# A graph layer with attention and experts: a prologue with other statistics, another load order and other places for the padding records

## What is computed

```
xn = layernorm(x)                                          # per row, over 512
x  = x + gnn(xn, src, dst, ...) + mix(xn)                  # mix: 8-head linear attention, softmax of q and of k
x  = x + experts(layernorm(x))                             # router, top 2 of 8 experts
# gnn: 40,000 edges
xs, xv  = xn[:, :128] @ W_in2f_s, xn[:, 128:] (3 x 128) @ W_in2f_v   # the node table
h       = shifted_softplus(f_ij @ Wf1 + bf1)               # f_ij: 20 features of the edge
W       = (h @ Wf2 + bf2) * rcut
message = products of xs[idx_j], xv[idx_j], u = r_ij/|r_ij| and W
agg     = segment_sum(message, idx_i)                      # idx_i = src: 1250 receiving nodes, unsorted
```

## Time and profile before

| | |
|---|---|
| median of 3 runs | 1466.07 us (1460.82 to 1468.56) |
| profiled execution, device time | 1465.51 us |
| its span | 1463.8 us |
| busy: PE, DVE, ACT, POOL | 1270.0, 1148.5, 819.3, 922.6 us |
| granted TensorE clock, mean | 0.938 |

### The profile page before, as it was taken

The page is one execution under the profiler, slowest core; times in us unless marked ns, Lnnn a source line. Parts: engine busy times, 40 slices in busy tenths (PEclk is TensorE's granted clock), DMA queues, the critical chain, the costliest instruction groups (busy, mean ns, idle before and its releaser), DMA issues.

```text
span 1463.8 us, 16076 instructions
## 1 busy us (share of the span) xinstructions
PE 1270.0 (87%) x4215; PEld 731.3 (50%) x4215; DVE 1148.5 (78%) x2117; ACT 819.3 (56%) x1777; POOL 922.6 (63%) x834
## 2 busy tenths in 40 slices
PE   3968878889888888699999999999999998885993
PEld 2655556666666655334444444444444443674871
DVE  6876547777777798569999999999999998367325
ACT  2355545666666656146667666666767655454330
POOL 7336666666666667568888888888888842143215
PEclk8979889999999999999999999999999999987995
DMA  8116656656656866588888888888888854434447
GB/s 247 49 66 249 238 200 249 244 201 256 243 223 258 311 210 237 210 303 292 306 297 297 290 294 298 298 306 297 299 293 292 286 175 121 173 130 169 162 130 213
DMA packets 104542, 344.51 MB, mean 235 GB/s; under 512 B 16501, under 2 KB 17437, under 8 KB 94469
## 3 DMA queue, kind: packets, MB, share of 16 engines
q0 software_dynamic: 58496, 192.21, 37.6%
q1 hardware_dynamic: 45956, 151.29, 28.3%
HBM read 216.63 MB, written 126.80 MB: 235 GB/s over the span
## 4 chain that ended last, share of the span: by engine, by line
PE 70%; DVE 12%; issue 6%; ACT 4%; another core or an unknown queue 4%; POOL 2%; DMA 2%; DVEq 0%; ACTq 0%; POOLq 0%
PE PS L2040 20%; PE PS L2045 18%; PE PS L1976 12%; PE PS L2165 5%; DVE RR L1350 3%; PE PS L1854 2%; PE PS L1935 2%; PE PS L1864 1%; PE PS L1943 1%; PE PS L1917 1%; POOL expert_inputs L832 1%; ACT RR L1029 1%; PE PS L2184 1%; PE PS L1974 1%
## 5 line engine op out<-in xcount | busy, mean ns | idle before, releaser
L799 POOL DMA_INDIRECT RR<-node_table,RR x332 | 470.6, 1418 | 144.3 <-issue 92.5
L1029 ACT ACTIVATE RR<-RR 128x256 f32<-128x256 f32 x996 | 407.2, 494 | 227.8 <-PE PS L2045 195.9
L783 POOL DMA_INDIRECT edge_records<-RR x316 | 325.8, 1031 | 190.3 <-issue 83.1
L2040 PE MATMUL PS<-RR 128*125 128x512 f32 x664 | 303.6, 599 | 20.2 <-issue 11.1
L2045 PE MATMUL PS<-RR 128*125 128x512 f32 x664 | 299.3, 592 | 0.0
L1350 DVE TENSOR_TENSOR RR<-PS,RR 128x512 f32<-128x512 f32 x237 | 161.8, 686 | 127.7 <-PE PS L1976 74.7
L2040 PEld LDWEIGHTS PS<-RR 128*125 128x125 f32 x664 | 117.8, 187 | 199.9 <-issue 186.2
L2045 PEld LDWEIGHTS PS<-RR 128*125 128x125 f32 x664 | 124.6, 188 | 160.3 <-issue 160.3
L1976 PE MATMUL PS<-wf_high,h_high 128*128 128x512 f32 x316 | 155.7, 493 | 22.0 <-DVE RR L1350 13.1
L1523 DVE TENSOR_TENSOR RR<-RR 128x1536 f32<-128x1536 f32 (+1 forms) x88 | 145.9, 1658 | 0.0
L1976 PE MATMUL PS<-wf_low,h_high 128*128 128x512 f32 x316 | 131.4, 416 | 0.0
(11 more groups left out here) (338 smaller groups left out, 1884.4 us busy)
## 6 DMA issues: line engine op xcount, KB each, us to landing
RR<-edge_records SPq DMA_DIRECT2D x78, 1040.0 KB
expert_inputs<-RR SPq DMA_DIRECT2D x8, 2560.0 KB
RR<-in_L_ffn_beta_w SPq DMA_DIRECT2D x8, 1024.0 KB
expert_w_raw<-in_L_ffn_expert_w SPq DMA_DIRECT2D x8, 1024.0 KB, 7.3
expert_outputs<-RR SPq DMA_DIRECT2D x27, 256.0 KB
edge_records<-RR POOLq DMA_INDIRECT x332
RR<-node_table,RR POOLq DMA_INDIRECT x332
RR<-edge_records SPq DMA_DIRECT2D x10, 520.0 KB
```

Source lines behind the costliest of these rows:

```text
L783: g.indirect_dma_start(out=rec_dram, out_offset=place, in_=ST[:, j, :], in_offset=None).then_inc(scattered[c], 16)
L799: g.indirect_dma_start(out=GB[:, q % GBS, t, 1:5, :].rearrange("p k n -> p (k n)"), out_offset=None, in_=tab_dram, in_offset=bass.Indirect ...
L1029: last = a.activation(message_slot(q)[:, t, k:k + 5:4, :], GB[:, q % GBS, t, 0:k + 3:k + 2, :], ACT.Copy, scale=record_slot(q)[:, t, 4 * C ...
L2040: te.matmul(PS[0:NT, b, :], OH[:, q % OHS, t, 0:NT], GB[:, q % GBS, t, 1:5, :].rearrange("p k n -> p (k n)"), start=(t == 0), stop=(t == n ...
```

## The change

- x is loaded in three parts: tiles 0 and 1, tiles 2 to 5 ahead of WV, tiles 6 to 9 behind WV.
- For tiles 2 to 9 ScalarE takes the statistics: a Copy with scale -1/512 whose accumulator gives minus the mean, and a Square with that as bias whose accumulator gives 512 times the variance. The square root then scales and adds epsilon. VectorE takes the reciprocals for tiles 2 and 3, 4 and 5, 6 to 9 apart.
- The masks of `count_block` are kept (`block_mask`), and COUNT_TILE is 7.
- `list_pairs` becomes `places_in_blocks`: ten operations on the kept masks in place of 19.
- `add_base` and POOL's share of it are gone. ScalarE makes for each tile a diagonal matrix of its offsets, and TensorE adds up ten products diagonal times mask in one PSUM bank, after the ten tiles of x; `pair_places` adds that bank once.
- `spare_places` moves from VectorE to POOL (without is_ge and the reduction), ahead of all scatters. Nine padding scatters come ahead of step 0, the other seven at steps 10, 20, ..., 70.
- The order ahead of step 0 differs on ScalarE, VectorE and TensorE, as below.

```diff
+        in_hidden = 4 * 512 // RC1
+        mask_at = [hidden_at + b * RC1 if b < in_hidden else kn_at + (b - in_hidden) * RC1 for b in range(NB)]
+        offset_diag = [w[:, 0:P] for w in (tC, tD)]
+        OFFSET_BANK = 6
+        block_mask = [R1[:, w:w + RC1] for w in mask_at]
-        COUNT_TILE = 4
+        COUNT_TILE = 7
-        EMPTY_STEP = 2
+        SPARE_FIRST = 9
+        spare_step = [10 * (n + 1) for n in range(NCOL - LOOPED - SPARE_FIRST)]
   # SP
+            load_x(slice(2, 6), x_in[1])
             load_projection(WV, Wv, wqkv_in[2])
-            load_x(slice(2, NB), x_in[1])
+            load_x(slice(6, NB), x_in[2])
   # POOL
-            pool.wait_ge(pairs_placed, 1)
-            for b in range(NB // 2, NB):
-                dest = tD if b > NB // 2 else tC
-                step(g.tensor_scalar(dest, bkt, float(b), off[:, b:b + 1], ALU.is_equal, ALU.mult))
-                if b > NB // 2:
-                    step(g.tensor_tensor(tC, tC, tD, ALU.add))
-            pool.sem_inc(pairs_listed, 1)
-            pool.wait_ge(places_ready, 1)
+            def spare_places():
+                pool.wait_ge(spare_bases, 1)
+                step(g.tensor_tensor(passed, kd.unsqueeze(2).to_broadcast([P, SPARE, 2 * NB]),
+                                     cpad.unsqueeze(1).to_broadcast([P, SPARE, 2 * NB]), ALU.subtract))
+                step(g.tensor_scalar(passed, passed, 0.0, 1.0, ALU.max, ALU.min))
+                step(g.tensor_tensor(passed, passed, fill.unsqueeze(1).to_broadcast([P, SPARE, 2 * NB]), ALU.mult))
...
+                g.tensor_copy(posi[:, RC1:NCOL], pd[:, 1:SPARE]).then_inc(places_ready, 1)
+            spare_places()
+            for n in range(SPARE_FIRST):
+                spare_record(LOOPED + n)
             for m in range(STEPS):
                 scatter(m // RING, m % RING)
-                if EMPTY_STEP <= m < EMPTY_STEP + NCOL - LOOPED:
-                    spare_record(LOOPED + m - EMPTY_STEP)
+                if m in spare_step:
+                    spare_record(LOOPED + SPARE_FIRST + spare_step.index(m))
   # ScalarE
+            def moments_of(ts):
+                for t in ts:
+                    a.activation(b2_rows[0:NT, :], X[0:NT, t, :], ACT.Copy, scale=-1.0 / D,
+                                 accum_out=mean[0:NT, t:t + 1]).then_inc(moments, 1)
+                for t in ts:
+                    act.wait_ge(moments, t - 1)
+                    a.activation(bb[0:NT, :], X[0:NT, t, :], ACT.Square, bias=mean[0:NT, t:t + 1],
+                                 accum_out=var_eps[0:NT, t:t + 1]).then_inc(squares, 1)
             table_rows(0)
+            act.wait_ge(x_in[1], 32)
+            moments_of((2, 3))
+            later_std(slice(2, 4), 3)
+            moments_of((4, 5))
+            later_std(slice(4, 6), 5)
             values(0)
             table_rows(1)
+            evac_xT(2)
             values(1)
-            std_of(slice(2, NB), 1)
-            act.wait_ge(nrm_sq, 1)
-            a.activation(inv, ssq, ACT.Sqrt).then_inc(nrm_root, 1)
-            evac_xT(2)
+            act.wait_ge(x_in[2], 32)
+            moments_of((6, 7))
             for t in range(2, NB):
                 table_rows(t)
                 if t + 1 < NB:
                     evac_xT(t + 1)
+                if t == 2:
+                    moments_of((8, 9))
+                    later_std(slice(6, NB), NB - 1)
                 values(t)
-                if t == 4:
+                if t == 5:
+            def offset_diagonal(b):
+                if b >= 2:
+                    act.wait_ge(diag_used, b - 1)
+                a.activation(offset_diag[b % 2], ident[:, :], ACT.Copy, scale=off[:, b:b + 1]).then_inc(diag_ready, 1)
+            act.wait_ge(spare_bases, 1)
+            for b in range(NB):
+                offset_diagonal(b)
...
             log_part(0, 0)
+            log_part(0, 1)
+            act.wait_ge(diag_used, NB)
+            high(0, 0)
             stage_f(3)
             radial(0, 2)
-            log_part(0, 1)
             stage_f(4)
             radial(0, 3)
             log_part(0, 2)
-            high(0, 0)
   # VectorE
-            for t in range(3):
-                count_block(t)
-            statistics(range(2, NB), 1)
-            inverse_root(range(2, NB), 1)
+            count_block(0)
+            inverse_root(range(2, 4), 1)
             normal(2)
             normal(3)
...
+                        step(v.scalar_tensor_tensor(srcf, block_mask[b], packed[:, b:b + 1], srcf, ALU.mult, ALU.add))
...
             def stage(i, c):
+                if (i, c) == (0, 0):
+                    dve.wait_ge(places_ready, 1)
...
             stage_f_low(0, 2)
+            hidden(0, 0)
             pair_places()
+            hidden(0, 1)
             stage_f_low(0, 3)
-            hidden(0, 0)
-            spare_places()
-            hidden(0, 1)
-            stage_f_low(0, 4)
             dve.wait_ge(b2_ready, 1)
             low(0, 0)
+            stage_f_low(0, 4)
   # TensorE, after the ten tiles
+            for b in range(NB):
+                pe.wait_ge(diag_ready, b + 1)
+                te.matmul(PS[:, OFFSET_BANK, 0:RC1], offset_diag[b % 2], block_mask[b], start=(b == 0), stop=(b == NB - 1))\
+                    .then_inc(diag_used, 1)
...
             layer1(0, 0)
+            layer1(0, 1)
             transposes(0, 2)
-            layer1(0, 1)
             transposes(0, 3)
```

More of the change, by code:

```diff
@@ L1159, in normal @@
                 v.tensor_scalar(XN[0:NT, t % XNS, :], X[0:NT, t, :], mean[0:NT, t:t + 1], rstd[0:NT, t:t + 1],
-                                ALU.subtract, ALU.mult).then_inc(xn_ready, 1)
-            step(v.memset(half[:, :], 0.5))
+                                ALU.subtract if t < 2 else ALU.add, ALU.mult).then_inc(xn_ready, 1)
+            v.memset(eps_col, EPS)
+            step(v.memset(half[:, 0:1], 0.5))
             statistics(range(0, 2), 0)
@@ L1179, in count_block @@
             def count_block(t):
-                step(v.tensor_scalar(tA, bkt, float(t), None, ALU.is_equal))
-                step(v.tensor_tensor_scan(tB, ones[:, 0:RC1], tA, 0.0, ALU.mult, ALU.add))
+                mask = block_mask[t]
+                step(v.tensor_scalar(mask, bkt, float(t), None, ALU.is_equal))
+                step(v.tensor_tensor_scan(tB, ones[:, 0:RC1], mask, 0.0, ALU.mult, ALU.add))
                 v.tensor_copy(cnt[:, t:t + 1], tB[:, RC1 - 1:RC1]).then_inc(counts_ready, 1)
-                step(v.tensor_tensor(tA, tA, tB, ALU.mult))
-                step(v.tensor_tensor(rnk, rnk, tA, ALU.add))
+                step(v.tensor_tensor(tC, mask, tB, ALU.mult))
+                step(v.tensor_tensor(rnk, rnk, tC, ALU.add))
             def block_bases():
@@ L1209, in block_bases @@
                 step(v.scalar_tensor_tensor(fill[:, 0:NB], ngf, float(GROUP), tot, ALU.mult, ALU.min))
-                v.scalar_tensor_tensor(off, pref, -1.0, first[:, 0:NB], ALU.add, ALU.add).then_inc(pairs_placed, 1)
+                v.scalar_tensor_tensor(off, pref, -1.0, first[:, 0:NB], ALU.add, ALU.add)
                 step(v.tensor_tensor(fill[:, NB:2 * NB], tot, fill[:, 0:NB], ALU.subtract))
@@ L1213, in block_bases, with places_in_blocks @@
                 step(v.tensor_tensor(cpad, first, filled, ALU.subtract))
-                step(v.tensor_tensor(cpad, cpad, fill, ALU.add))
-            def add_base(b):
-                step(v.tensor_scalar(tA, bkt, float(b), off[:, b:b + 1], ALU.is_equal, ALU.mult))
-                step(v.tensor_tensor(rnk, rnk, tA, ALU.add))
-            def list_pairs():
+                v.scalar_tensor_tensor(cpad, cpad, -1.0, fill, ALU.add, ALU.add).then_inc(spare_bases, 1)
+            def places_in_blocks():
                 for b in range(NB):
-                    dest = tA if b else srcf
-                    step(v.tensor_scalar(dest, bkt, float(b), packed[:, b:b + 1], ALU.is_equal, ALU.mult))
                     if b:
-                        step(v.tensor_tensor(srcf, srcf, tA, ALU.add))
+                        step(v.scalar_tensor_tensor(srcf, block_mask[b], packed[:, b:b + 1], srcf, ALU.mult, ALU.add))
+                    else:
+                        step(v.tensor_scalar(srcf, block_mask[b], packed[:, b:b + 1], None, ALU.mult))
             def pair_places():
-                dve.wait_ge(pairs_listed, 1)
-                step(v.tensor_tensor(rnk, rnk, tC, ALU.add))
                 step(v.tensor_copy(srci, srcf))
@@ L1236, in pair_places @@
                 step(v.scalar_tensor_tensor(srcf, tB, -float(P), srcf, ALU.mult, ALU.add))
+                dve.wait_ge(diag_used, NB)
+                step(v.tensor_tensor(rnk, rnk, PS[:, OFFSET_BANK, 0:RC1], ALU.add))
                 v.scalar_tensor_tensor(tA, srcf, float(GROUP), rnk, ALU.mult, ALU.is_le)
@@ L1312, in _ @@
             block_bases()
-            list_pairs()
-            for b in range(NB // 2):
-                add_base(b)
+            places_in_blocks()
             def stage(i, c):
```

(2 more changed lines are left out.)

75 lines of the change are left out of this document (50 added, 25 removed).

## The result

The changed kernel takes 1449.24 us in the median (1448.73 to 1451.24, 4 runs) where the kernel before takes 1465.13 (1460.82 to 1468.56, 4 runs): ratio 0.9916, 95% interval 0.9888 to 0.9945, 15.9 us less. The forecast was 1458 with 1446 to 1468. The profiled execution spans 1449.5 us, 14.3 less than before.

The account below looks back on a forecast made before the run. It took VectorE's chain, with TensorE's ten tiles close, to bound the prologue and neither engine to pace the steps. Prologue -5.7 and padding scatters -2 gave -7.7 on 1465.5: 1457.8, median 1458, range 1446 to 1468.

Parts of the forecast that it names:

- What bounds the kernel: Prologue: VectorE alone from 61.4 to 88, TensorE's ten tiles close behind; in the steps neither sets a steady pace.
- Load order, clock, TensorE's ten tiles: Prologue: WV at 16.3, 4.0 us later; half clock costs 2 us; TensorE's tiles end at 66.7, 10.4 us earlier.
- ScalarE's statistics: Prologue: first eight end by 19, hidden; later ones cost TensorE 1 us; VectorE loses 6.1 us of statistics.
- VectorE up to the block bases, and POOL beside it: Prologue: bases done at 63.4, places_in_blocks at 68.6 to 71; POOL adds at most 4.3 us, costing nothing.
- The offsets by TensorE: TensorE after tile 9: ten offset products take 6.0 us; bias rows start at 73.8, 4.2 us earlier, not 10.4.
- From T to the first column: From T, the start of the bias rows, to ScalarE's first column: T + 15.9, at 89.7, 5.7 us earlier.
- Padding scatters: POOL: nine scatters ahead end at 81 to 85, costing nothing; the steps gain 2 us, between -17 and +9.
- rival 1: Steps: early ones were slow because of padding scatters, most of the 17 us comes too, about 1445; chance 0.17.
- The most that it can bring: Steps: 16 early ones took 7.35 us each, 60 later ones 6.29; 16 x 1.06 = 17 us as upper bound.
- The second: Prologue: half clock, offset products and ScalarE's statistics eat the gain on TensorE, about 1466; chance 0.20.
- The fourth: First stage: POOL's places come late if spare_places takes over 23 us; about 2 in 100, inside the third.
- The third: Steps: stalls without a releaser fall elsewhere, three more of the longest give 1475; chance 0.13 with the fourth.

Follow-up runs that it names:

- first experiment and its repetition: Changed kernel with all 16 padding scatters back in steps 2 to 17, none ahead: 1459.0 us, ratio 0.9970; repeated 1378.87 us, ratio 0.9969.
- with all ahead: Changed kernel with all sixteen padding scatters ahead of step 0, none in the steps: 1434.27 us, ratio 0.9800; repeated 1369.18 us, ratio 0.9897.

## Why the prediction came out as it did

**What bounds the kernel.** Right for the prologue. For the steps it said that neither engine sets a steady pace. That was read where stalls of up to 5.8 us cover the pace; without them POOL and TensorE are both full.

**Load order, clock, TensorE's ten tiles.** Value product 16.41 (16.3 said), tile 2's transposes 26.77 (26.3), offset products from 68.12 (67.8). After 4.7 us of idleness the granted clock was 0.50 from 16.4 to 21 and 1.00 from 22.5 on: the 2 us taken were spent there. WV's 4.0 us at the start were right too, but they are no net cost of the load order: with WV first TensorE loses as much later (0.5 us between the two).

**ScalarE's statistics.** The accumulator costs an instruction of its own, 0.19 us, near the upper bound of 0.21. Eight operations ahead of the first values ended at 19.8 (19 said), hidden as said. VectorE was spared the 6.1 us, but by the experiment with the statistics on VectorE again that is worth 1.1 to 2.2 us at the end. With the statistics of tiles 2 and 3 on VectorE, tile 2's transposes still start at 27.94 without a wait: it is mostly the order of the work (statistics of later tiles not ahead of tile 2's scaling) that closed the hole of 13.9 us, and not that ScalarE took them.

**VectorE up to the block bases, and POOL beside it.** Bases at 57.99 to 62.3 (63.4 said). The nine additions of places_in_blocks took 0.72 us each beside POOL and not 0.49; 0.23 more is within the 0.43 that the prediction allowed from the earlier trace rows, and it stayed hidden in the 7.1 us that VectorE then stood:

```profile
62.63 6.50 DVE L1286 SCALAR_TENSOR_TENSOR RR<-RR,small 128x313 f32<-128x313 f32 x9
...
76.23 0.32 DVE L1331 TENSOR_TENSOR feature_columns<-RR,feature_columns 128x160 fp32r<-128x160 f32 x1 [7.11 <-issue]
```

**The offsets by TensorE.** Bias rows at 74.2 (73.8), 6.4 us for the products (6.0). "The offsets give six of them back" was right, and the experiment with the offsets on VectorE puts a price on it: 5.8 us of the whole kernel.

**From T to the first column.** 89.79 (89.7 said), and the kernel's time followed: 6.0 us with stalls and 5.0 without are the prologue's share (first experiment and its repetition), where 5.7 were forecast.

**Padding scatters.** This is the term that was mis-sized: -2 taken from -17 to +9; measured -9.8 with stalls and -5.0 without. The step that failed is "VectorE never waited ahead of stage for a landing in this trace, so POOL's 1.27 are not on the path themselves". The wait was absent in that trace, and what was read from its absence was too much. POOL's own column should have been added up, by the start times: four scatters at 1.265 are 5.06 us a step, with a padding scatter 6.33, and the 60 later steps went at 6.29. So with a padding scatter POOL could not have kept the pace of the later steps. Steps 2 to 17 took more than that, 7.35, and POOL waited in them as well, 19.2 us in all beyond the 0.30 between two scatters, most of it for VectorE:

```profile
POOL edge_records L783 <- DVE RR L1350: 11.9, 7, 3.2
POOL edge_records L783 <- DVE RR L1323: 8.9, 8, 3.9
```

A turn costs the more the less of it falls into such a wait. The prediction's own sign for rival 1, steps 2 to 17 at the pace of the later ones, came out (6.22 against 6.47). "The most that it can bring", 17 us from the two paces, was no forecast either: sixteen turns came to 9.7 us without stalls, because half of each fell into POOL's waits. That the time still fell into the range is in part luck: the term for the prologue was right, and the one for the padding stood near zero between two far bounds.

**The rivals.** The first has the right mechanism and a smaller size (5 to 10 us for its part, not 15), though its argument against, that no wait ends on it, was mine for -2. The second fell: clock 1.00 in the offset products. The fourth fell: the places were ready at 70.0, long before the first stage. The third, stalls that fall elsewhere, is not excluded for the kernel with stalls. The "remote" waits of VectorE and ScalarE in steps 2 to 17 came to 43.6 us before, 52.6 with the scatters back, 16.0 in the changed kernel and 2.8 with all ahead. But over the whole filter stage they came to 117, 124, 120 and 66: from the kernel before to the changed one they did not get fewer, they lie later. So part of what steps 2 to 17 won and the later steps lost is stalls that moved. What releases them the traces don't say: the engines stand together for 4 to 6 us, the same code on a chip with the same number has none of them at another time, and no kernel here tells a cause. For the time with stalls, what speaks for POOL's turns is that the first-to-last time of the scatters grew by 8.7 us for nine and shrank by 8.5 for seven, in one profile each; how much of the 15.9 us is stalls that fell otherwise stays open.

## What to carry to other kernels

Add up a queueing engine's column by the distance between the starts of its instructions, not by its busy time, and compare that with the pace of the loop in each stretch; a wait that doesn't show up in one trace is no proof of slack, because buffers hide a late engine for many steps and then the wait shows on another engine. Before work is moved from one engine to another, look at what the first does afterwards: VectorE, relieved of the block offsets, stood for 7 us, and TensorE, which got them, was on the path. A gain in a shared loop should be measured at more than one level of disturbance if it can be had.

## What the runs showed of the hardware

- An indirect scatter of 128 records took POOL 0.96 us busy in most cases (1.00 in the mean without stalls) and 0.30 us until the next started, 1.265 us apart, with 260 KB behind each; without stalls the same bytes from SP's queue, one write a step, cost the kernel nothing that could be seen (0.3 us).
- ScalarE's accumulator output is an instruction of its own, 0.18 to 0.19 us.
- VectorE's scalar_tensor_tensor on 313 columns took 0.72 us beside POOL's tensor operations, 0.58 mostly without them, and 0.48 to 0.49 with none of them beside it. The Trainium skill, page "SBUF — State Buffer", section Who interferes with whom, has an instruction with two SBUF inputs contend with one of GpSimd that reads SBUF. The trace agrees, with 0.72 against 0.49 us.
- The same kernel took 1465 us at one time and 1383 at another, 5.6% less, on a chip with the same number. The profiles of the slower time have stalls of 4 to 6 us on several engines at once in the loop of steps, and that loop holds nearly all of the difference (72.3 of 76.7 us in the changed kernel). That the stalls make up all of it is not shown: with all sixteen ahead steps 2 to 17 have only 2.8 us of them and still take 6.05 us each, 5.43 at the faster time.
